# Issuing the k rows of every batch from ACT's queue, one slot behind their split

## The reference

```python
# layer 0
xm = layernorm(x, g1, be1) * (1 + sc_a) + sh_a
q, k, v = split(xm @ Wqkv)                       # 16 heads of 16
attn = softmax(where(causal, q @ k.T * 0.25, -inf))
x = x + gt_a * ((attn @ v) @ Wproj + bproj)
xm = layernorm(x, g2, be2) * (1 + sc_m) + sh_m
x = x + gt_m * (gelu(xm @ W1 + b1) @ W2 + b2)
# layer 1: the same shape, adaln in place of gains, biases on q, k, v, a mask
# of whole key columns in place of the causal one, no gates
```

## Time and profile before

| | |
|---|---|
| time, median of 3 runs | 1189.88 us (1187.13 to 1192.58) |
| profiled execution: its own time, its span | 1188.98 us, 1186.9 us |
| PE busy | 1094.0 us (92% of the span), 9228 matmuls |
| PE's weight loads busy | 959.8 us |
| DVE, ACT, POOL busy | 747.9, 624.0, 253.1 us |
| mean granted clock of PE | 0.974 of full speed |
| attention of layer 0, MLP, attention of layer 1, MLP | about 44 to 400, 400 to 605, 605 to 985, 985 to 1183 us |

### The profile page before, as it was taken

One profiled execution on the slowest core, in us unless ns is written; L12 is line 12 of the kernel. 1 busy time (PEld: TensorE's weight loads), 2 busy tenths in 40 slices (PEclk: granted clock), 3 DMA queues, 4 the chain that ended last, 5 costly groups with the idle time before them and its releaser, 6 DMA issues.

```text
span 1186.9 us, 24117 instructions
## 1 busy us (share of the span) xinstructions
PE 1094.0 (92%) x9228; PEld 959.8 (81%) x9228; DVE 747.9 (63%) x1627; ACT 624.0 (53%) x1255; POOL 253.1 (21%) x252
## 2 busy tenths in 40 slices
PE   3889999999999789999975899999999987999998
PEld 3778899998987578899874788888888765998997
DVE  5456666666665466655635777878777747556653
ACT  1146666666665633433422677767777676334431
POOL 5101221211211343223321121121211113111111
PEclk9789999999999998999987999999999999999999
DMA  7647767567661110000057554736547300001001
GB/s 214 113 67 113 131 107 119 102 106 117 145 97 30 19 41 9 10 9 14 15 88 151 85 80 69 95 60 88 77 75 92 57 2 1 19 20 35 19 19 36
DMA packets 50826, 81.49 MB, mean 69 GB/s; under 512 B 8916, under 2 KB 23476, under 8 KB 49620
## 3 DMA queue, kind: packets, MB, share of 16 engines
q1 hardware_dynamic: 49752, 78.37, 37.9%
q10 hardware_dynamic: 960, 1.57, 1.2%
HBM read 22.64 MB, written 8.44 MB: 26 GB/s over the span
## 4 chain that ended last, share of the span: by engine, by line
PE 72%; SPq 9%; DMA 9%; DVE 4%; issue 3%; ACT 2%; POOL 2%; ACTq 1%; POOLq 0%; DVEq 0%
PE st_bank L541 13%; PE g_bank L541 11%; SPq L406 8%; PE o_bank L541 8%; PE s_bank L541 7%; PE o_bank L629 7%; DMA k_stack<-qk_split 5%; PE s_bank L590 3%; PE s_bank L596 3%; PE st_bank L615 3%; DMA k_stack<-mask_dram 3%; PE st_bank L611 2%; PE st_bank L609 2%; PE s_bank L592 2%; PE g_bank L687 2%
## 5 line engine op out<-in xcount | busy, mean ns | idle before, releaser
L807 ACT ACTIVATE probs<-st_bank 128x384 f32<-128x384 f32 (+1 forms) x512 | 276.6, 547 | 152.6 <-PE st_bank L611 83.2
L541 PE MATMUL st_bank<-qk_split,q_stack 128*128 128x512 f32 x768 | 190.1, 406 | 14.4 <-ACT probs L910 9.8
L910 ACT ACTIVATE probs<-st_bank,cols 128x512 f32<-128x512 f32 x128 | 88.0, 689 | 219.4 <-PE st_bank L541 193.8
L1099 DVE TENSOR_REDUCE maxima<-s_bank 128x2 f32<-128x512 f32 x256 | 168.8, 684 | 51.0 <-PE s_bank L596 50.8
L541 PEld LDWEIGHTS st_bank<-qk_split,q_stack 128*128 128x128 f32 x768 | 146.9, 194 | 52.7 <-ACT probs L910 13.1
L1095 DVE TENSOR_REDUCE maxima<-s_bank 128x3 f32<-128x384 f32 x256 | 136.8, 552 | 65.6 <-PE s_bank L592 62.1
L596 PE MATMUL s_bank<-k_stack,q_stack 97*128 97x256 f32 x512 | 117.1, 311 | 26.7 <-DMA k_stack<-mask_dram 14.5
L541 PE MATMUL g_bank<-xmT,wa 128*128 128x256 f32 x768 | 123.1, 300 | 4.8 <-POOL xmT L1271 4.8
L629 PE MATMUL o_bank<-probs,v_sb 128*32 128x256 f32 (+1 forms) x2048 | 123.4, 358 | 1.6 <-ACT probs L807 1.6
L596 PEld LDWEIGHTS s_bank<-k_stack,q_stack 97*128 97x128 f32 x512 | 78.8, 192 | 55.6 <-issue 41.5
L1271 POOL TENSOR_TENSOR xmT<-xm_full,xmT 128x512 fp32r<-128x512 f32 x32 | 42.2, 1320 | 332.2 <-ACT xmT L873 332.2
(11 more groups left out here) (114 smaller groups left out, 2129.5 us busy)
## 6 DMA issues: line engine op xcount, KB each, us to landing
q_stack<-qk_split SPq DMA_DIRECT2D x192, 128.0 KB, 4.4
k_stack<-qk_split SPq DMA_DIRECT2D x180, 128.0 KB, 6.2
gate_rows<-gate_dram SPq DMA_DIRECT2D x32, 128.0 KB, 3.0
w_dram<-w_in SPq DMA_DIRECT2D x8, 512.0 KB, 7.6
wm_f32r<-w_dram SPq DMA_DIRECT2D x4, 1024.0 KB, 8.4
out<-x_sb SPq DMA_DIRECT2D x8, 512.0 KB, 2.9
x_sb<-x_in SPq DMA_DIRECT2D x4, 512.0 KB, 7.9
k_stack<-qk_split ACTq DMA_DIRECT2D x12, 128.0 KB, 8.4
```

The source lines that it names most:

```text
L541: last = mm(dst, weights[i], rows[j], start=(f == 0 and n == 0), stop=(f == tiles - 1 and n == len(TERMS) - 1))
L807: activation(probs[:, h % 8, 0:n], st_bank[h % 2][:, 0:n], ACT.Exp, scale=SCALE)\
L910: activation(h_full[:, m % 2], st_bank[m % 2][:, :], ACT.Gelu, bias=cols[:, cb + m:cb + m + 1])\
L1099: v.reduce_max(maxima[:, gb.mod(2), 0:2, slot], bank[:].rearrange("p (i n) -> p i n", n=T), AX.X).then_inc(max_done, 1)
```

## The change

The six k DMAs of every batch, not of batch 0 alone, are issued by ACT, in slot 6 (batch 0 had them in slot 5); SP's are gone. ACT waits there for `k_lo`.

```diff
@@ SP, step(layer, t)
                     restack(q_stack, q_split, g, (0, 1, 0), q_stacked)
-                    if a.const > 0:
-                        when(k_lo, g.count(1, 1))
-                        restack(k_stack, k_split, g, (0, 0, 1), k_stacked)
                     if layer == 1:
@@ ACT, step(layer, t), after the exponentials of slot s and the splits
-                    if s == SLOT["k"][1] and a.within(B) and a.const == 0:
-                        act.wait_ge(k_lo, ga.count(1, 1))
+                    if s == SLOT["k"][1] + 1 and a.within(B):
+                        wait_apart(act, k_lo, ga.count(1, 1), act_passed)
                         for half in (0, 1):
                             for row, e in enumerate((0, 0, 1)):
                                 p = HALF * half + HD * row
```

More of the change, by code:

```diff
@@ L245, in build @@
         power_set = sem("power_set")
-        sp_passed, dve_passed, pool_passed = sem("sp_passed"), sem("dve_passed"), sem("pool_passed")
+        sp_passed, dve_passed, pool_passed, act_passed = (sem(f"{e}_passed") for e in ("sp", "dve", "pool", "act"))
         var_shifted = sem("var_shifted")
```

## The result

The changed kernel takes 1275.09 us (median of 4 runs, 1271.13 to 1278.03), the one before 1188.57 (4 runs, 1187.13 to 1192.58): a ratio of 1.0706, 95% interval 1.0676 to 1.0736. The forecast was 1246, its range 1215 to 1288. The profiled execution is the fastest of the four, 1271.13 us with a span of 1268.9, which is 82.0 more than before's 1186.9; its mean granted clock is 0.947, before 0.974.

What follows compares the result with a forecast made beforehand. PE was taken to bound full steps. Stalls of 22.9 and 33.2 us plus 8.3 for disturbed issues, less 7.3 regained, made 57.1 us on 1188.98: forecast 1246 us, 8-in-10 range 1215 to 1288.

Steps and rivals of the forecast that it cites:

- What bounds the kernel: Full steps: PE is the bound, busy all 21.45 us in layer 0; what holds it up mid-step is not given back.
- What it removes: SP's six k issues, 3.76 us, go; layer 1's full-step waits for k_stack, 7.3 us, are regained, bounds 0 and 28.9.
- ACT is held for 3.9 us and PE for 1.76 and 2.39: Full steps: six issues delay ACT's copy of o_sb, so PE stalls 1.76 us in layer 0, 2.39 in layer 1.
- The added 0.16 for the copy of v: Layer 1 full step: PE's second transposes start at 788.77, not 788.61, bringing the stall from 2.39 to 2.55 us.
- plain stalls: PE's stalls in 13 full steps per layer: 13 x 1.76 = 22.9 us and 13 x 2.55 = 33.2 us.
- disturbed issues: Some six-issue groups exceed 3.76 us, as on SP; on ACT this is uncovered, 8.3 us, bounds 0 and 31.7.
- So most should stay at the upper level: After stalls of 1.8 and 2.5 us, or 3.0 to 3.7 disturbed, PE's clock mostly stays at 2.4 GHz.
- a rival of 17%: PE's clock falls in the stalls, 1.6 us each in 13 to 26 steps: 1267 to 1288 us; chance 17%.
- Two queues, one at a time: Only one of SP's q and ACT's k queues issues at once, holding ACT 1.9 us longer: 1295 us; chance 6%.
- The prediction's own sign: Sign of being wrong: a group of issues on ACT takes over 5 us while SP issues q.
- Filling steps at nothing: Steps 1 to 3 of each layer: ACT's 3.90 us hold is covered by PE's k_stack waits; uncovered, some 9 us.

Runs made afterwards that it cites:

- the spread one: Changed kernel with the six k DMAs on ACT placed one at the end of each of slots 6 to 11: 1201.63 us, 1.0078 of before.
- five on ACT: Changed kernel with one of the six k DMAs of every batch back on SP behind q's: 1242.74 us, 1.0396 of before.
- ACT held: Kernel before, k DMAs still on SP; ACT waits for k_lo, then runs two long activations into a scratch tile: 1257.59 us, 1.0544 of before.

## Why the prediction was right, and where it was off

- **What bounds the kernel.** Right. PE is the bound in full steps, and a stall in the middle of one isn't given back: 23.43 us for a step of layer 0, which had 21.45.
- **What it removes.** The gain in layer 1 came as forecast, 7.3 us of waits to none. It is worth no more than that.
- **ACT is held for 3.9 us and PE for 1.76 and 2.39.** Right in mechanism, and the main term. The issues behind DVE's low part took 3.91 to 4.08 in the rows above, and began 0.11 us behind it, not 0.03; the stalls are 1.76 and 2.22 in them. The added 0.16 for the copy of v does not show as a wait. Summed, PE waited 55.5 us in the 26 full steps, where 56.1 for the plain stalls and 8.3 for disturbed issues make 64.4.
- **Where the stalls were too high, and luck.** The issues themselves came as forecast: the 26 groups sum to 107.7 us, forecast were 26 x 3.90 + 8.3 = 109.7. But a stall is the group less the slack before PE needs the copy, and that was larger: 4.08 - 1.76 = 2.32 us in layer 0 and 3.91 - 2.22 = 1.69 in layer 1, where the forecast has 2.14 and 1.51. That 1.76 was forecast and 1.76 measured in layer 0 is luck: the group there took 4.08, and groups of 3.82 and 3.83 gave stalls of 1.50 to 1.54.
- **"So most should stay at the upper level"** is the step that failed. It put the fall of the clock into a rival of 17%, and the sum has no term for PE running slower. In layer 1 the clock fell in 12 of 13 stalls, and PE was busy for 20.7 us longer in the full steps: 1.7 us a fall, the three long ones among them. In layer 0 it is 8.6 us, of which four falls, at 24.97 - 23.43 = 1.54, are 6.2. The price for one (1.6) was about right, the count in layer 1 wasn't. The argument leaned on one wait of 2.4 us with the clock still up, and took one case for the usual. The trace of the kernel before had another case, in the MLP stage, where the clock is down behind a wait of 1.77 us:

```profile
445.63 2.27 PE L541 MATMUL st_bank<-qk_split,q_stack 128*128 128x512 f32 x5 [1.77 <-ACT probs L910]
...
446.00:450.00 4.00, 3.47 (x9) 2.27 (x8) 3.93 (x7) 1.37 (x2) 2.73 (x3) 0.50 0.00 0
```

The Trainium skill, "TensorE: Matmul & The Clock Gate", HAM oscillation — how this bites in real kernels, describes this pattern, a wait in each tile and each tile starting cold. Here it came with waits of 2.2 us, in one layer and hardly in the other.

- **Two queues, one at a time.** Did not come true: forecast for it were 3.9 + 1.9 us, and 18 of the 26 groups took 3.8 to 4.1 us beside SP's of q. The prediction's own sign, a group over 5 us while SP issues q, came once there (5.19 us, at 786 us) and once while layer 1 fills (6.09 us, at 667 us). Before the change SP had groups of 5.19 and 5.39 with nothing issued on ACT, so the first tells nothing of two queues; the second stays open.
- **Bulk loads beside k's** were in no part of the prediction. They cost the changed kernel 3.1 us of waits and a fall of the clock, covered otherwise by the stalls, and the spread one 14.8 us of waits and two falls.
- **Filling steps at nothing.** About right: outside the full steps the span grew by 2.4 us. But the waits there did not stay as they were: those for k_stack fell from 21.6 to 8.9 us, and PE's for the copy of v rose from 9.5 to 14.9 and for exponentials (L606 and L612 now) from 1.5 to 7.6.

The account: in the full steps PE's idle time grew by 50.3 us, where the forecast has 57.1 (8.9 less for the stalls, 3.1 more for the waits at L587, and 1.0 of smaller waits gone), and its busy time by 29.3, where the forecast has nothing. About 27 of these are the 16 falls of the clock. The other 2 or so lie in layer 0, 0.2 us a step with the clock up (21.64 us busy in the first stretch above, 21.45 in the earlier trace rows), and were not taken apart. With 2.4 outside the full steps that makes the 82.0 us. The time of 1275 lies near the middle of the rival's 1267 to 1288, so it was that case that came, in one layer of two.

## What to carry to other kernels

A DMA costs the queue that issues it some 0.65 us, and on an engine that also computes everything behind it in its order waits for that, so count the issues, find what stands behind them, and ask when it is needed: three issues all but fitted into ACT's slack here, five and six did not, and one per slot did. A stall of PE is worth more than its length once the clock falls with it; with five DMAs in place of six, stalls shorter by 17 us in all came with 32 us of time. And a second queue is also a way past the first: what was issued behind a short transfer in one queue runs beside it in two.

## What the runs showed of the hardware

- **The clock in repeated stalls.** By the length of the usual stall in a step of some 22 to 24 us: 1.1 us (five on ACT, layer 0), the clock fell in 0 of 13; 1.61 (ACT held), in 1; 1.5 to 1.8 (changed), in 3, one of them behind a stall of 2.34; 1.55 to 1.9 with two of 2.9 (five on ACT, layer 1), in 6; 2.2 (changed, and ACT held), in 12. In the changed kernel's layer 0 a stall of 2.57 us had no fall and one of 1.75 had. The layers differ in the work around the stall too, so it isn't shown that length alone decides.
- **An issue overlaps the activation ahead of it.** With the six behind the copy of o_sb they began at 217.24, 0.08 us after that activation of 0.39 us had started, and 0.08 or 0.09 after it in all 26 full steps, but nothing behind them began before 221.25.
- **POOL issued the same six in 3.23 us** by its rows of the profile, which are rough on POOL, and in two of 32 steps stood over 7 us between the third and the fourth; ACT and SP took 3.76 to 3.91 where nothing disturbed them.
